# One more chunk of attention probabilities turned by way of DRAM, in place of TensorE, in two of four row tiles

## The reference

```python
# attention, on the layer-normed rows of x; the cached keys and values are both ctx (512 per batch)
q = x_n @ wq.T;  k = concat(ctx, x_n @ wk.T);  v = concat(ctx, x_n @ wv.T)
attn = softmax(q @ k.T / sqrt(512))                    # 512 rows x 1024 keys per batch
x = x + tanh(g_xattn) * (attn @ v) @ wo.T
# feed-forward with signs of the weights, 512 -> 2048 -> 512, on the layer-normed rows of the new x
h = relu(layernorm(x) @ sign(up).T * up_scale)
x = x + tanh(g_ffn) * (h @ sign(down).T * down_scale) * output_scale
```

## Time and profile before

| what | value |
|---|---|
| median of 3 runs | 579.07 us |
| the profiled execution | 578.94 us |
| its span, first to last instruction | 577.1 us |
| mean granted TensorE clock | 0.999 |
| TensorE matmuls busy | 571.5 us, 99% |
| VectorE / ScalarE / GpSimd busy | 397.4 / 281.1 / 125.7 us |

### The profile page before, as it was taken

One profiled execution on the slowest core, in us unless ns is written; L12 is line 12 of the kernel. 1 busy time (PEld: TensorE's weight loads), 2 busy tenths in 40 slices (PEclk: granted clock), 3 DMA queues, 4 the chain that ended last, 5 costly groups with the idle time before them and its releaser, 6 DMA issues.

```text
span 577.1 us, 6906 instructions
## 1 busy us (share of the span) xinstructions
PE 571.5 (99%) x2610; PEld 474.7 (82%) x2610; DVE 397.4 (69%) x556; ACT 281.1 (49%) x402; POOL 125.7 (22%) x111
## 2 busy tenths in 40 slices
PE   9999999999999999999999999999999999999997
PEld 7888888888888888888888888888888888888885
DVE  5889646688685588683588686777569645766654
ACT  3783513464321564321565454756468355555531
POOL 5006222102033002033002033332322022422002
PEclk9999999999999999999999999999999999999999
DMA  8711752124414145425113833273910311330011
GB/s 290 244 69 33 187 182 74 35 75 109 111 65 82 40 180 146 109 76 73 57 53 104 247 124 109 92 164 110 212 44 36 147 37 37 108 112 36 6 67 74
DMA packets 93248, 59.97 MB, mean 104 GB/s; under 512 B 71840, under 2 KB 75936, under 8 KB 92832
## 3 DMA queue, kind: packets, MB, share of 16 engines
q1 hardware_dynamic: 93216, 59.54, 35.4%
HBM read 44.84 MB, written 14.69 MB: 103 GB/s over the span
## 4 chain that ended last, share of the span: by engine, by line
PE 97%; DVE 1%; DMA 0%; ACT 0%; issue 0%
PE proj L680 28%; PE score L796 20%; PE turn L781 13%; PE score L714 9%; PE score L680 8%; PE turn L680 8%; PE proj L781 5%; PE proj L714 4%; PE score L922 2%; PE turn L672 1%; PE score L672 1%; DVE rows L1787 1%; DMA rows<-in_x 0%; DVE scaled L1784 0%; DVE stats L1615 0%; PE score L929 0%
## 5 line engine op out<-in xcount | busy, mean ns | idle before, releaser
L796 PE MATMUL score<-down_signs,hid_split 128*128 128x512 f32 x512 | 133.3, 389 | 0.0
L796 PEld LDWEIGHTS score<-down_signs,hid_split 128*128 128x128 f32 x512 | 96.0, 188 | 20.3 <-DVE hid_split L1668 0.5
L680 PE MATMUL proj<-four_x,weights 128*128 128x512 f32 x336 | 76.8, 389 | 0.0
L680 PEld LDWEIGHTS proj<-four_x,weights 128*128 128x128 f32 x336 | 63.0, 188 | 13.0
L604 POOL TENSOR_TENSOR four_x<-raw_ctx,four_x 128x2048 fp32r<-128x2048 f32 x7 | 32.6, 4656 | 132.0 <-ACT four_x L1010 132.0
L1668 DVE TENSOR_TENSOR hid_split<-hid,hid_split 128x512 fp32r<-128x512 f32 x64 | 44.4, 697 | 15.4 <-ACT hid_split L1226 15.1
L781 PE MATMUL turn<-ops_b,up_ops 128*128 128x512 f32 x192 | 51.3, 389 | 0.0
L1226 ACT ACTIVATE hid_split<-hid 128x512 fp32r<-128x512 f32 x64 | 40.0, 629 | 20.8 <-PE score L796 17.9
L1217 ACT ACTIVATE hid<-hid,hid_gain 128x512 f32<-128x512 f32 x48 | 34.7, 724 | 22.7 <-DVE hid L1697 11.1
L680 PE MATMUL score<-weights,four_x 128*128 128x512 f32 x192 | 45.3, 389 | 0.0
L680 PE MATMUL proj<-weights,four_x 128*128 128x512 f32 x192 | 45.3, 391 | 0.0
(11 more groups left out here) (140 smaller groups left out, 928.1 us busy)
## 6 DMA issues: line engine op xcount, KB each, us to landing
raw_w<-in_ffn_w SPq DMA_DIRECT2D x21, 512.0 KB, 3.3
raw_ctx<-in_ctx_turned SPq DMA_DIRECT2D x4, 1024.0 KB, 5.3
raw_ctx<-in_ctx SPq DMA_DIRECT2D x4, 1024.0 KB, 6.5
probs_rows<-probs_squares SPq DMA_DIRECT2D x64, 64.0 KB, 1.9
squares_placed<-probs_rows SPq DMA_DIRECT2D x8, 512.0 KB, 4.2
raw_x<-block_rows SPq DMA_DIRECT2D x4, 1024.0 KB, 7.3
result<-rows SPq DMA_DIRECT2D x16, 256.0 KB, 2.1
rows<-in_x SPq DMA_DIRECT2D x3, 1024.0 KB, 9.3
```

The source lines that it names most:

```text
L680: last = pe.matmul(bank, lhs(l), rhs(r), start=start and i == 0, stop=stop and i == 2)
L796: last = pe.matmul(wide(r), hid_split[:, n % HR, s, r * P:(r + 1) * P], down_signs[:, chunk_of(q), :], start=(q == 0 and s == HI), stop=(q ...
```

## The change

- Of tiles 2 and 3, the squares now take five chunks of keys (640 columns) instead of four: the four of the old keys and chunk 4, the first of the new. TensorE transposes three chunks of these tiles instead of four. Tiles 0 and 1 stay at four and four. (`FAR`, `FAR_ALL`.)
- The store of a square block of tiles 2 and 3 has 20 x 32 runs instead of 16 x 32; the first part that is loaded back has five chunks instead of four, and so have its high and its low half.
- SyncE loads the first part after the stores of the third tile (0), ahead of the stores of the fourth (1).
- The squares lie at 112 KB, where the queries' operands (`qT`, `raw_q`) lay. The first `square_probs` of a batch waits for the last product of A22 instead of that of S1. `placed_out` of part 0 no longer waits for the stores of part 1.
- The new terms: chunk 4's term comes last. For each e terms 1, 2, 3 run first; then TensorE waits for part 0 (`placed_lo` 2b+1), and term 0 of the four e follows. In e = 0, the third product is now that of v3 and has its wait.

```diff
+        FAR = {2: RT + 1, 3: RT + 1, 0: RT, 1: RT}
+        FAR_ALL = RT + 1
-        probs_squares = at("probs_squares", 160, [P, RT, ROWS])
+        probs_squares = at("probs_squares", 112, [P, RT, FAR_ALL * P])
...
-            return slice(None), slice(0, RT), slice(first, first + 2 * P)
+            return slice(None), slice(0, FAR[PAIRS[h][0]]), slice(first, first + 2 * P)
...
+                for t in TILE_ORDER[:3]:
+                    store_tile(t)
                 sp.wait_ge(scored, product_scored(b, A22, 1))
-                for h, pair in enumerate(PAIRS):
-                    sp.wait_ge(squares_stored[h], 2 * STORED * (b + 1))
-                    cols = slice(pair[0] * P, (pair[1] + 1) * P)
-                    sp.dma_start(squares_placed[placed_part(h)], probs_rows_v[b][:, :, cols]).then_inc(placed[h], 16)
+                place(0)
+                store_tile(TILE_ORDER[3])
+                place(1)
...
-                turn_job(turn0(b) + i, cols(probs[:, t, ROWS:KEYS]))
+                turn_job(turn0(b) + i, cols(probs[:, t, FAR[t] * P:KEYS]))
...
-                    for i, (lhs, rhs) in enumerate(new_terms(e)):
+                    for i, (lhs, rhs) in enumerate(new_terms(e)[1:]):
                         if e == 0:
-                            pe.wait_ge(proj_lo, values_out(b, max(i, 2)))
+                            pe.wait_ge(proj_lo, values_out(b, max(i + 1, 2)))
                         last = product(proj_bank(n + DC + e), lhs, rhs, i == 0, False)
+                pe.wait_ge(placed_lo, 2 * b + 1)
+                for e in range(DC):
+                    last = product(proj_bank(n + DC + e), *new_terms(e)[0], False, False)
...
             def placed_out(b, h):
                 act.wait_ge(placed[h], 16 * (b + 1))
-                if h == 0:
-                    act.wait_ge(squares_stored[1], 2 * STORED * (b + 1))
...
                 if t == TILE_ORDER[0]:
-                    dve.wait_ge(scored, product_scored(b, S1, 1))
-                dve.transpose(probs_squares[:, t, :], probs[:, t, 0:ROWS]).then_inc(probs_squared, 1)
+                    dve.wait_ge(scored, product_scored(b, A22, 1))
+                dve.transpose(probs_squares[:, t, 0:FAR[t] * P], probs[:, t, 0:FAR[t] * P]).then_inc(probs_squared, 1)
```

More of the change, by code:

```diff
@@ L160, in gated_block @@
         late_squares = normed
+        FAR = {2: RT + 1, 3: RT + 1, 0: RT, 1: RT}
+        FAR_ALL = RT + 1
         PAIRS = ((2, 3), (0, 1))
-        probs_squares = at("probs_squares", 160, [P, RT, ROWS])
+        probs_squares = at("probs_squares", 112, [P, RT, FAR_ALL * P])
         squares_placed = at("squares_placed", 176, [P, KC, ROWS])
-        probs_rows = nc.dram_tensor("probs_rows", (BATCH, ROWS, ROWS), F32).ap()
+        probs_rows = nc.dram_tensor("probs_rows", (BATCH, FAR_ALL * P, ROWS), F32).ap()
         probs_rows_v = probs_rows.rearrange("b (c p) q -> b p c q", p=P)
@@ L232, in turn_bank, with turned_cols @@
             return turn[:, n % 4, :] if n % 4 < 2 else score[1][:, n % 4 - 2, :]
+        def turned_cols(n):
+            return 4 * P if n < RT else KEYS - FAR[TILE_ORDER[n % RT]] * P
         def proj_bank(n):
@@ L451, in place_squares, with store_tile, place @@
             def place_squares(b):
-                for h, pair in enumerate(PAIRS):
[L454 to L458, removed]
+                def store_tile(t):
+                    sp.wait_ge(probs_squared, tile_done(b, t))
+                    far = FAR[t] * P // SQ
+                    for i in range(P // SQ):
+                        sp.dma_start(probs_squares_v[b, t, i][:, 0:far],
+                                     probs_squares[i * SQ:(i + 1) * SQ, t, 0:far * SQ].rearrange("n (j a) -> n j a", a=SQ)
+                                     ).then_inc(squares_stored[t not in PAIRS[0]], 16)
+                def place(h):
+                    sp.wait_ge(squares_stored[h], 2 * STORED * (b + 1))
+                    first, last = PAIRS[h]
+                    sp.dma_start(squares_placed[placed_part(h)],
+                                 probs_rows_v[b][:, 0:FAR[first], first * P:(last + 1) * P]).then_inc(placed[h], 16)
+                for t in TILE_ORDER[:3]:
+                    store_tile(t)
                 sp.wait_ge(scored, product_scored(b, A22, 1))
-                for h, pair in enumerate(PAIRS):
-                    sp.wait_ge(squares_stored[h], 2 * STORED * (b + 1))
-                    cols = slice(pair[0] * P, (pair[1] + 1) * P)
-                    sp.dma_start(squares_placed[placed_part(h)], probs_rows_v[b][:, :, cols]).then_inc(placed[h], 16)
+                place(0)
+                store_tile(TILE_ORDER[3])
+                place(1)
             def block_rows_back(b):
@@ L675, in cols @@
             def cols(src):
-                return [src[:, k * P:(k + 1) * P] for k in range(4)]
+                return [src[:, k * P:(k + 1) * P] for k in range(src.shape[1] // P)]
             def product(bank, lhs, rhs, start, stop):
@@ L1013, in turn_out @@
                 act.wait_ge(turned, n + 1)
-                act.activation(dst, four(turn_bank(n)), ACT.Copy).then_inc(turn_hi, 1)
+                act.activation(dst, four(turn_bank(n)[:, 0:turned_cols(n)]), ACT.Copy).then_inc(turn_hi, 1)
             def proj_out(n, dst):
@@ L1095, in probs_out @@
                 t = TILE_ORDER[i]
-                turn_out(turn0(b) + i, probsT[:, HI, RT:KC, t * P:(t + 1) * P])
+                turn_out(turn0(b) + i, probsT[:, HI, FAR[t]:KC, t * P:(t + 1) * P])
             def placed_out(b, h):
@@ L1303, in turn_out @@
                 dve.wait_ge(turn_hi, n + 1)
-                dve.tensor_tensor(dst(LO), four(turn_bank(n)), dst(HI).bitcast(F32), ALU.subtract
+                dve.tensor_tensor(dst(LO), four(turn_bank(n)[:, 0:turned_cols(n)]), dst(HI).bitcast(F32), ALU.subtract
                                   ).then_inc(turn_lo, 1)
@@ L1387, in probs_out @@
                 t = TILE_ORDER[i]
-                turn_out(turn0(b) + i, lambda s: probsT[:, s, RT:KC, t * P:(t + 1) * P])
+                turn_out(turn0(b) + i, lambda s: probsT[:, s, FAR[t]:KC, t * P:(t + 1) * P])
             def square_probs(b, t):
```

## The result

The changed kernel takes 580.58 us (median of 12 runs, 579.86 to 582.18) against 579.08 us (12 runs, 578.88 to 579.49): ratio 1.0027, 95% interval 1.0020 to 1.0035. It is slower by 1.5 us, just beyond the 0.2% that counts as a change. The forecast was +1.0 us and 580.1, inside the range; the case "slower" had 0.36 and "no change" 0.60. The profiled execution is one of the fastest: 579.87 us, with a span of 578.0 us, 0.92 more than before's.

A forecast was written before the change was run, and what follows sets the result against it. TensorE, busy for 571.5 of 577.1 us, was taken to bound the kernel. Per batch -0.22 + 0.14 + 0.33 = +0.25, four batches +1.0 us: 579.94, and against the median 580.07, forecast 580.1; range 578.7 to 581.0.

The forecast's parts named there:

- TensorE's list sets the time: Whole kernel: time is the sum of what TensorE issues; edits elsewhere count only where they make TensorE wait.
- Term 1: TensorE's transposes at L672: two fewer per batch, at 0.109 us each, shorten its list by 0.22 us a batch.
- Term 2: Tile 1's exponentials come 0.27 us later behind larger squares on VectorE; TensorE stands 0.14 us a batch (0 to 0.22).
- Term 3: New terms, e = 0: v3's wait comes one product earlier, so TensorE stands 0.33 us a batch (0.27 to 0.44).
- The sign named for it: At tile 1's transposes: a new TensorE wait at L672 on ScalarE's `probs` L1091, four times, some 0.14 us each.
- The sum: All four batches: -0.22 + 0.14 + 0.33 = +0.25 us each, +1.0 us in all; bounds +0.2 to +1.8.
- The step that failed: SyncE's queue behind the change: context, next rows and feed-forward weights come later but were put at nothing.
- Part 0's new wait: Old terms' wait on `placed_lo` 2b+1: part 0 ready 1.1 to 4 us early in batch 3, costing nothing.
- Full gain: Rival: the waits at v3 and tile 1 don't show, -0.87 us, 578.2; chance 0.14, including near it.
- whole-duration transposes: Rival: each transpose is worth its 0.273 us duration, -2.2 us; 578.7 with both stalls, 576.9 without; chance 0.04.
- Part 0 late: Rival: part 0's load is late and TensorE waits at the new wait; 581.7 or 586.5 us; chance 0.08.

The follow-up runs named there:

- experiment 7: Changed kernel with v3's wait behind 12 matmuls, the fourth tile's stores first, and tile 3's squares behind tile 1's maxima: 579.94 us, three runs 577.92 to 578.24.
- experiment 3: Kernel before, with the first transpose of tiles 2 and 3 done twice, eight transposes more in all: 579.91 us against 579.01.
- experiment 2: Kernel before, with only the new order of the new terms, all four chunks still transposed by TensorE: 580.36 us, ratio 1.0022.
- experiment 1: Changed kernel, with the new terms reordered so that v3's wait stands 12 matmuls behind the first load and not 6: 579.22 us, 1.36 less.
- experiment 4: Changed kernel, with the fourth tile's four stores ahead of the load of part 0 again: 579.95 us, 0.63 less than the changed kernel.
- experiment 5: Changed kernel with four chunks in all tiles' squares and the old order of new terms; part 0's load still ahead of the fourth tile's stores: 578.86 us.
- experiment 11: Kernel before, with SyncE in batch 0 waiting for part 0's high half ahead of the next rows' load and the facts' store: 579.12 us, ratio 1.0005.
- e9: Changed kernel, with batch 0's small store of the next batch's row_facts moved right behind part 0's load: 587.96 us, ratio 1.0157.
- e10: Changed kernel with v3's wait moved, fourth tile's stores first, tile 3's squares behind tile 1's maxima, batch 0's row_facts stored between both loads: 586.04 us.

## Why the prediction was right, and where its size was off

- **TensorE's list sets the time.** It held: terms 1 and 3 came out of experiments within 0.1 us of their size, term 2 out of the trace and of three runs of experiment 7. The forecast came out 0.5 us low for something else, which it had put at nothing (below).
- **Term 1**, 0.22 us a batch for two transposes: 0.90 us for eight (experiment 3), against 0.87. The 640-column squares took 832 ns, for some 835.
- **Term 2**, 0.14 us a batch for tile 1's exponentials. Mis-sized: 0.08. The squares (127 ns for 135), the end of the exponentials (58.03 for 58.04) and the load's lateness (58.08, where 57.52 + 4 x 0.109 = 57.95 was its turn: 0.13 for 0.14) came as forecast. The sign named for it didn't: no list of TensorE's waits names L1109; the gap between the loads is 0.09 us (57.99 to 58.08). But tile 1's loads, once they go, catch up:

```profile
57.52 0.47 PEld L686 LDWEIGHTS score<-ident,probs 128*128 128x128 f32 x4
...
58.08 0.42 PEld L686 LDWEIGHTS score<-ident,probs 128*128 128x128 f32 x4
```

  Four loads of tile 0 take 0.47 us, the four late ones 0.42. I had counted cover for the late load of term 3 and none for this one.
- **Term 3**, 0.33 us a batch for v3: 0.35 to 0.38 in the trace (0.44 late for 0.43, and 0.08 covered for 0.10), 1.32 and 1.36 us for four by experiments 2 and 1. This was the term that decided the sign, and it came from nothing else than putting the end of one instruction beside the start of a load.
- **The sum** with the measured terms is 579.0 - 0.87 + 0.32 + 1.32 = 579.8. The profiled execution, 579.87, is that within 0.1. The runs' median is 0.7 above. The forecast also took the 1.84 us outside the span as fixed; five of 12 runs had 0.5 more there.
- **The step that failed** is the sentence that what SyncE issues behind "serves work some microseconds off; TensorE shows no wait there now". I had worked out the cover for part 0 and part 1 in batch 3 and none for batch 0's queue behind them. Nor was the delay right: 0.5 to 1.8 us were allowed, and part 1's load came 2.9 us later in batch 0 and 4.7 in batch 3, where the fourth tile's stores, now behind a load of 640 KB, landed after 4.4 to 4.9 us in place of 1.9. Part 1's low half ended at 333.45 for the 332 allowed at most, and was in time by 0.6 us only because TensorE was 0.9 later too. In batch 0 a chain of a store, two loads and four operations hangs on it, with next to no cover left in the changed kernel: in its first profile the first keys were out at 101.54 + 0.57 = 102.11 and wanted at 96.83 + 24 x 0.2265 = 102.27, in its second they were late. By the same working the cover is 1.7 us in the kernel before and in experiment 4, 0.6 in experiment 5 and 0.2 in experiment 11, of which three runs in 11 were 0.7 us longer. It takes the load ahead of the stores and the fifth chunk together: with either alone (experiments 4 and 5) the spans lie within 0.5 us.
- **Part 0's new wait** costs nothing in any profile with the facts in their old place, as forecast; the load at 72.35 has no idle time before it, and in batch 3 part 0 was ready 2.4 us early, inside the 1.1 to 4 allowed.
- **Rivals.** Full gain fell with experiments 2 and 1, whole-duration transposes with 3. By the Trainium skill ("TensorE: Matmul & The Clock Gate", Part 4: PE-mode transpose) a transpose takes about 275 ns in a kernel and is dominated by its latency; the trace agrees with the duration of one (272 ns) and shows that a row of them doesn't add up by it (+0.90 us for eight). What dominates the one no run here shows. Part 0 late did not occur in the changed kernel's profiles.

## What to carry to other kernels

Where one engine is busy for 99%, a reordering of its products is not free: put the end of each awaited instruction beside the start of the load that waits, at the new place, for each wait that moves. And of a queue that is changed, follow every transfer behind the change to its last reader, in the batch with the least cover, not only in the one where the change is aimed at. An engine's gain of 0.9 us was real here; a wait that moved by one product and exponentials that came 0.26 us later took 1.6 back, and the queue's order 0.6 (experiment 4).

## What the runs showed of the hardware

- A store of 4 KB in 1024 runs of 4 bytes took 11.9 to 15.1 us to landing in batch 0 of the profiles. Four stores behind it in the queue landed after 11.3 to 12.6 us in place of 3.8 to 4.3 (e9), and a load issued 0.5 us ahead of it after 10.6 (e10). Its place in the queue matters more than its 4 KB suggest.
- Eight transposes of 272 ns each lengthen TensorE's list by 0.90 us.
- A wait on the weight load is partly covered: 0.44 us late at the load is 0.36 in the list of 512-column matmuls, 0.13 late is 0.08 in a row of transposes.
- After 6.9 us without work TensorE's granted clock was 0.50 for 6 us more, with 14 matmuls of 512 columns (some 0.43 us each) where 26 would pass at 0.2265 (e9).
